# ScalarE's queue in a recurrence: a decay and the second pair of weighings change places

## The reference

```python
def step(state, inp):                       # L0_attn, D_IN = 1024, N = 16
    dt_t, B_t, C_t, u_t = inp
    dA = jnp.exp(dt_t[..., None] * A)
    state = state * dA + (dt_t * u_t)[..., None] * B_t[:, None, :]
    y = jnp.einsum('bdn,bn->bd', state, C_t)
    return (state, y)
```

## Time and profile before

| | |
|---|---|
| median of 3 runs | 1420.16 us (1419.8 to 1423.55) |
| profiled execution | 1422.61 us, its span 1420.8 us |
| granted TensorE clock, mean | 0.972 |
| busy: PE, DVE, ACT, POOL | 1295.8, 927.6, 730.9, 646.1 us |
| scans, L1649 | 256, first at 136.4 us, last at 504.9 us |
| weighings on ACT | 448, mean 495 ns |
| decays | 256, mean 727 ns |

### The profile page before, as it was taken

How to read it: one execution, slowest core, us unless ns; L and a number is a source line. 1 busy time by engine, 2 the same in 40 slices (tenths; PEclk the granted TensorE clock), 3 DMA queues, 4 the chain that set the end, 5 groups by cost and what they waited for, 6 DMA issues and landing times.

```text
span 1420.8 us, 18312 instructions
## 1 busy us (share of the span) xinstructions
PE 1295.8 (91%) x6432; PEld 932.2 (66%) x6432; DVE 927.6 (65%) x1690; ACT 730.9 (51%) x1407; POOL 646.1 (45%) x471
## 2 busy tenths in 40 slices
PE   6996887888899889989999997999999999999996
PEld 5874665666667654444655553778877788878874
DVE  4775899988888977895534434544444465555566
ACT  5489998899888831121222222544444434444341
POOL 4129988889878702216511112633333343333221
PEclk9998999999999999999999996999999999999999
DMA  5002200030000060012010000322212122111110
GB/s 173 8 24 89 90 1 1 31 148 1 1 1 0 1 181 15 15 53 97 9 30 8 0 15 30 112 67 75 68 66 75 45 81 76 64 64 61 51 52 30
DMA packets 29641, 71.45 MB, mean 50 GB/s; under 512 B 3408, under 2 KB 3664, under 8 KB 27632
## 3 DMA queue, kind: packets, MB, share of 16 engines
q1 hardware_dynamic: 29552, 70.30, 14.9%
HBM read 68.12 MB, written 2.16 MB: 49 GB/s over the span
## 4 chain that ended last, share of the span: by engine, by line
PE 66%; DVE 14%; ACT 10%; issue 5%; POOL 3%; DMA 1%; SPq 1%; DVEq 0%; POOLq 0%; ACTq 0%
PE psum L493 9%; PE psum L495 9%; PE psum L494 9%; ACT arena L951 6%; DVE arena L1649 4%; PE psum L568 4%; PE psum L899 4%; PE psum L769 4%; PE psum L926 4%; PE psum L763 3%; ACT psum L951 3%; PE psum L593 3%; PE psum L918 2%; PE psum L582 2%; PE psum L663 2%
## 5 line engine op out<-in xcount | busy, mean ns | idle before, releaser
L1649 DVE TENSOR_TENSOR_SCAN arena<-psum,arena 128x512 f32<-128x512 f32 x256 | 298.7, 1208 | 49.1 <-ACT psum L951 49.1
L1381 POOL TENSOR_TENSOR arena<-arena 128x1024 f32<-128x1024 f32 x128 | 300.4, 2369 | 46.7 <-DVE arena L1649 46.5
L1317 POOL TENSOR_TENSOR w_split<-arena,w_split 128x512 fp32r<-128x512 f32 x128 | 168.1, 1331 | 311.9 <-ACT w_split L951 311.8
L568 PE MATMUL psum<-prm,arena 128*128 128x128 f32 x1024 | 167.2, 289 | 67.5 <-DVE arena L1649 44.1
L568 PEld LDWEIGHTS psum<-prm,arena 128*128 128x128 f32 x1024 | 115.4, 144 | 136.6 <-DVE arena L1649 68.3
L951 ACT ACTIVATE arena<-psum,ssmC 128x256 f32<-128x256 f32 x448 | 179.5, 495 | 45.3 <-PE psum L568 45.2
L951 ACT ACTIVATE arena<-arena 128x512 f32<-128x512 f32 (+2 forms) x86 | 64.1, 749 | 224.9 <-DVE arena L1916 224.0
L951 ACT ACTIVATE arena<-psum 128x512 f32<-128x512 f32 (+2 forms) x164 | 92.3, 575 | 169.3 <-PE psum L769 53.7
L951 ACT ACTIVATE psum<-arena,amat 128x508 f32<-128x508 f32 x256 | 170.9, 727 | 0.5 <-DVE arena L1649 0.5
L951 ACT ACTIVATE arena<-psum,prm 128x512 f32<-128x512 f32 (+1 forms) x130 | 90.4, 707 | 142.0 <-PE psum L495 77.4
L582 PE MATMUL psum<-prm,arena 128*128 128x128 f32 x1024 | 137.6, 278 | 0.1
(11 more groups left out here) (225 smaller groups left out, 2422.5 us busy)
## 6 DMA issues: line engine op xcount, KB each, us to landing
arena<-wq SPq DMA_DIRECT2D x64, 256.0 KB, 2.5
arena<-wo SPq DMA_DIRECT2D x64, 256.0 KB, 2.9
arena<-bc_scratch SPq DMA_DIRECT2D x8, 1024.0 KB, 4.8
arena<-win SPq DMA_DIRECT2D x16, 256.0 KB, 3.8
arena<-xT SPq DMA_DIRECT2D x8, 256.0 KB, 6.4
x_tok<-xtok SPq DMA_DIRECT2D x1, 2048.0 KB, 10.7
arena<-wout SPq DMA_DIRECT2D x8, 256.0 KB, 5.9
arena<-ctxtok SPq DMA_DIRECT2D x1, 2048.0 KB, 7.7
```

The source lines that it names most:

```text
L568: last = nc.tensor.transpose(hT[:, c, b % 2, e, :], hst[:, (2 * k + e) % 4, b * L:(b + 1) * L], ident)
L1317: gp.tensor_tensor(out_, whole, hi.bitcast(F32), ALU.subtract).then_inc(done, 1)
L1381: gp.tensor_tensor(bu[:, i % 4, :, :], dtu[:, (2 * j + e) % 4, :].unsqueeze(1).to_broadcast([P, NG, HT]), Brep[:, q * NG:(q + 1) * NG, :], ...
L1649: v.tensor_tensor_scan(hst[:, i % 4, :], bank[decay_slot(i)][:, :], bu[:, (k // NG * 2 + e) % 4, k % NG, :], 0.0, ALU.mult, ALU.add).then_ ...
```

## The change

In the old loop round k issues the decays 2k+2 and 2k+3, then the two pairs of weighings. Now three decays are issued ahead of the loop, and `weigh` itself issues decay 2k+3+c ahead of the pair c. The decay is issued also where the pair is DVE's. Nothing else is changed.

```diff
--- before.py
+++ after.py
@@ -1096,6 +1096,8 @@
             def weigh(k):
 
                 for c in range(2):
+                    if 2 * k + 3 + c < 2 * NR:
+                        decay(2 * k + 3 + c)
                     if by_dve(k, c):
                         continue
                     act.wait_ge(S.h_turned, 3 * k + 2 + c)
@@ -1108,12 +1110,9 @@
 
             for M in range(2):
                 skip_of(M)
-            for i in range(2):
+            for i in range(3):
                 decay(i)
             for k in range(NR):
-                if k + 1 < NR:
-                    decay(2 * k + 2)
-                    decay(2 * k + 3)
                 weigh(k)
                 if k % NS == 2 and k >= NS:
                     for e in range(2):
```

## The result

The changed kernel takes 1429.93 us (median of 8 runs, 1425.99 to 1433.74), the one before 1423.32 (median of 8 runs, 1419.8 to 1424.66, among them the three of the table at the head). The ratio is 1.005, 95% interval 1.0033 to 1.0067: some 7 us slower (6.6 by the medians, 4.7 to 9.5 by the interval), where +9 was forecast.

The account below looks back on a forecast made before the run. A loop of waits with no engine full, ACT's own work setting three rounds of four; +7, +1 and +1 gave +9 us, a median of 1429 from 1420.16, range 1419 to 1437 (own case 1424.5 to 1434).

Parts of the forecast that it names:

- one exchange, of D(2k+4) and P1(k): ACT's queue, round k: D a decay, P a weighing pair; only these two swap, in three rounds of four.
- The loop P1, four transposes, P0 at 2.92 us: Between ACT and PE: second weighing pair, four transposes, next first pair; three rounds of four take 2.92 us against 2.66.
- The fourth round, 2.54: The round in four where DVE weighs the second pair: 2.54 us against 3.04, a gain of 0.50.
- finish_y, 4.03: Once in 16 rounds, between two scans on DVE: its round takes 4.03 us against 3.70.
- The signs: In the profile after: first pairs wait 0.3 us for PE, DVE's decay waits nearly vanish, PE's weighing waits grow.
- Sixteen rounds, 46.3, and +7 for the first stretch: Rounds 4 to 84, cut at each round's first weighing, a(k): 46.3 us per sixteen against 44.97, five blocks, +7.
- Start, +1: First four rounds, PE at the lower clock: 12.3 us against 11.3, with 3.4 each for the first two.
- Late stretch, 132.0: Rounds 84 to 127: 132.0 us against 131.2, +1; possibly off by 4 us either way.
- the rival in which this stretch pays back: Rounds 84 to 127: DVE's slack absorbs LayerNorm parts and other delays, 5 us lower, total 1423.5; chance 0.16.
- the second part of the LayerNorm: DVE work in late rounds 103, 113 and 123: 0.9 us long, put at 0.7 us added in all.
- the two spells of the lower clock: PE at the lower clock in rounds 84 to 127: 0.75 us each as before, 1.5 together.
- The clock: Rival: PE, less busy, drops to 1.2 GHz in 80 rounds, 0.45 us each, +36, 1465 us; chance 0.06.

Follow-up runs that it names:

- e1: Kernel before, with decay 2k+4 moved ahead of the second pair only in rounds k mod 4 = 1: 1417.41 us, ratio 0.9969.
- e2: Kernel before, with decay 2k+4 moved ahead of the second pair only in rounds k mod 4 = 0 and 3: 1432.73 us, ratio 1.0069.
- e3: Changed kernel, with PE transposing the first half of both blocks, then the second half of both: 1412.53 us, ratio 0.9943 to the kernel before.
- e4: Kernel before, with PE's transposes ordered by halves and ACT's old order kept: 1422.54 us, ratio 1.0003.
- e8: e5 with finish_y also moved behind both scans: 1391.46 us, ratio 0.9781 to the kernel before.
- e6: e5 with ACT's old order, both decays after the second pair: 1414.57 us, ratio 0.9944 to the kernel before.
- e5: e3 with DVE's weighing moved behind both scans of the next round: 1401.04 us, ratio 0.9855 to the kernel before.

## Why the prediction was right

*The change is one exchange, of D(2k+4) and P1(k).* e1 and e2 take it apart by place, and each place behaves as its own.

*The loop P1, four transposes, P0 at 2.92 us.* Measured 2.92, the median in each of the three kinds of round. It is shown, and not only argued: with the order on PE that opens it, and the waits that go with that order, the same ACT queue goes back to 2.65 (e3), and that order does nothing without the early decays (e4).

*The fourth round, 2.54.* Measured 2.57, from 3.04. e1 shows that this gain hangs on the one early decay in the round before.

*finish_y, 4.03.* Measured 4.04.

*The signs.* P0(k) was to wait some 0.3 us for PE; the profile shows 0.17, and by starts it is 0.25. DVE's wait for decays was to vanish nearly, and half of it stayed, 10.9 us: I had not carried on that DVE, whose work has not grown, has to stop somewhere in a longer round. It costs nothing, so the time was not touched by this.

*Sixteen rounds, 46.3, and +7 for the first stretch.* Measured +9.0. From a(48) = 277.40 to a(64) = 323.86 it is 46.46, which over five blocks would be +7.4. The rest of the 9.0 is in spells of the lower clock behind finish_y: three of the five blocks have one, and in them the round after finish_y is 3.38 to 3.41 us instead of 2.92 and the DVE round in two 2.78 instead of 2.57. I had taken these to be as many as before. Before, two of the five had one, and one of the two cost nothing (rounds 65 and 66 take 5.64 us together, 5.65 elsewhere): the five blocks are 1.9 us over 5 x 46.46 now and were 0.3 over 5 x 44.97.

*Start, +1.* Measured +0.5. The first round was right (140.88 - 137.50 = 3.38 against 3.4), the second 2.92 against 3.4. I had reckoned it as 16 transposes at the lower clock, but the granted clock rose at 142.8 us, with eight of them to come. Windows:

```profile
125.70:142.80 17.10, 5.88 (x25) 4.80 (x26) 7.49 (x7) 15.11 (x22) 15.74 (x11) 0.50 0.16 61
142.80:149.00 6.20, 4.88 (x39) 3.96 (x38) 5.73 (x6) 5.48 (x12) 6.20 (x4) 1.00 0.52 190
```

PE's timeline:

```profile
141.06 1.89 PE L582 MATMUL psum<-prm,arena 128*128 128x128 f32 x8
142.76 1.22 PE L568 MATMUL psum<-prm,arena 128*128 128x128 f32 x8
143.82 0.93 PE L582 MATMUL psum<-prm,arena 128*128 128x128 f32 x7
```

From sums to sums PE needs 143.82 - 141.06 = 2.76, less than the loop.

*Late stretch, 132.0, called the least sure term.* Measured 131.7. LayerNorm behind rounds 105 and 125 is hidden wholly or to 0.1 us (2.92 and 3.03 where before 3.57), behind 95 costs 4.00 (4.02 by the sum), and the five rounds with both skip and output matmuls stay at 3.47. So the rival in which this stretch pays back was wrong. That the sum is so close is partly luck, since its items were off both ways: the second part of the LayerNorm costs nothing (2.92 in rounds 113 and 123) where 0.7 was put, and the two spells of the lower clock take more than the 1.5 put for them (round 96 is 4.81; rounds 115 and 116 are 4.25 and 4.00, where e2, without a spell, has 4.04, 4.01 and 2.92).

*The clock.* The granted clock in the first stretch is 0.98 as before. In e8 it is 1.00 over 205.65 us in which PE is busy 87% and does little but transposes. This contradicts, as the rows before the change did, what the Trainium skill says (TensorE: Matmul & The Clock Gate, "PE-mode transpose"), that the full clock does not engage for transposes.

The forecast of 1429 stands against a median of 1429.93, but that closeness owes something to luck in the base: the kernel before has a median of 1423.32 in its eight runs and of 1420.16 in the first three, on which the forecast stands. The difference is what was predicted, +9 against +7.

## What to carry to other kernels

An instruction moved forward in a queue moves the one that it passes backward; cost both, and follow the one that moved back to who stands behind it in order on the next engine. Where a single buffer makes two engines take turns, write out the loop and its length from rows: slack of 0.3 us under a busy engine can hide it, and a 0.6 us delay in it comes out in full above that slack. Before undoing such a change, look for the wait that the order on the neighbouring engine adds without need: here the same early decays lost 7 us with PE's transposes ordered by block and gained 8 with them ordered by half, and became worth more once DVE's weighing stood behind the scans (0.51 us per period between e6 and e5, 0.37 between e4 and e3).

## What the runs showed of the hardware beyond that

In the changed kernel short stretches at 1.2 GHz stand behind finish_y's pause in three of five places, and behind the same pause not in the others: PE's waits of 0.83 and 0.90 us in the round of finish_y are the same in all five. One of them, as a window of the changed kernel:

```profile
235.00:238.40 3.40, 2.91 (x15) 2.46 (x13) 2.41 (x3) 2.77 (x8) 2.42 (x2) 0.51 0.02 5
```

Each cost 0.5 to 0.7 us with the round that follows, as in the round at 234.29 that takes 3.38 us instead of 2.92. Further back, where nothing was changed, the profiled execution had 13.7 us at that clock from 648.0 on, and the one of before 6.8 us from 643.7 on. The eight runs of the changed kernel, one program, have mean granted clocks of 0.971 to 0.976 and lie 7.8 us apart: as much as the 7 us of this change, which only medians of several runs show.
